# Second self attention of a perceiver block: exponentials and scores by halves of a group's four heads

## The reference

```python
q = split_heads(x @ Wq); k = split_heads(x @ Wk); v = split_heads(x @ Wv)   # b=2, h=16, s=256, d=16
qc = q - q.mean(axis=-1, keepdims=True)
kc = k - k.mean(axis=-1, keepdims=True)
cov = jnp.einsum('bhsd,bhtd->bhst', qc, kc) / D
var_comp = q_var[..., :, None] * k_var[..., None, :] / D
attn = jax.nn.softmax(cov + var_comp, axis=-1)
out = jnp.einsum('bhst,bhtd->bhsd', attn, v)
```

## Time and profile before

| what | value |
|---|---|
| median of three runs | 1666.3 us |
| the profiled execution's own time | 1669.16 us |
| its span in the profile | 1667.4 us |
| mean granted clock of TensorE | 0.961 |
| the eight steps of this self attention, first score to last division | 1561.30 to 1591.05 us |

### The profile page before, as it was taken

One profiled execution on the slowest core, in us unless ns is written; L12 is line 12 of the kernel. 1 busy time (PEld: TensorE's weight loads), 2 busy tenths in 40 slices (PEclk: granted clock), 3 DMA queues, 4 the chain that ended last, 5 costly groups with the idle time before them and its releaser, 6 DMA issues. The chain is left out here.

```text
span 1667.4 us, 42036 instructions
## 1 busy us (share of the span) xinstructions
PE 1547.2 (93%) x15983; PEld 874.4 (52%) x15983; DVE 1105.6 (66%) x1794; ACT 890.1 (53%) x1208; POOL 697.5 (42%) x543
## 2 busy tenths in 40 slices
PE   7999999999899999999878969999999999997783
PEld 3554545544333444433453426777777777774442
DVE  4656566566789999997337756666666666625446
ACT  5555555554378888888251015555555555552435
POOL 5431000000011111111153009999999999971710
PEclk9999999999799999999899969999999999998897
DMA  7988979886832222221400067555565565311000
GB/s 235 228 229 229 210 218 228 234 231 158 223 99 67 68 68 65 65 66 35 162 2 1 5 176 229 152 156 135 158 161 142 137 161 159 86 40 59 2 1 13
DMA packets 178503, 212.23 MB, mean 127 GB/s; under 512 B 57381, under 2 KB 151857, under 8 KB 173769
## 3 DMA queue, kind: packets, MB, share of 16 engines
q1 hardware_dynamic: 177800, 210.44, 46.3%
q10 hardware_dynamic: 576, 0.00, 0.0%
HBM read 122.78 MB, written 87.57 MB: 126 GB/s over the span
## 5 line engine op out<-in xcount | busy, mean ns | idle before, releaser
L1231 POOL TENSOR_TENSOR x_r<-x_p 128x1024 f16<-128x1024 f32 x256 | 478.9, 1895 | 6.3
L1246 DVE TENSOR_REDUCE x_mx<-a_all 128x2 f32<-128x1024 f32 x249 | 304.9, 1225 | 150.9 <-PE a_all L1129 150.9
L1206 ACT ACTIVATE x_p<-s_all 128x1024 f32<-128x1024 f32 x256 | 248.4, 1022 | 227.0 <-PE s_all L1112 227.0
L802 ACT ACTIVATE x_p<-s_all 128x1024 f32<-128x1024 f32 x256 | 261.6, 1025 | 60.8 <-PE s_all L709 55.4
L850 DVE TENSOR_REDUCE x_mx<-a_all 128x1 f32<-128x512 f32 x352 | 231.9, 682 | 15.2 <-PE a_all L718 8.3
L1112 PE MATMUL s_all<-x_q,x_k 64*128 64x256 f16 x3072 | 210.2, 269 | 0.0
L1147 PEld LDWEIGHTS o_all<-x_v,x_p 128*128 128x128 bf16 x2048 | 178.7, 97 | 40.1 <-issue 40.1
L1147 PE MATMUL o_all<-x_v,x_p 128*128 128x129 f16 x2048 | 197.3, 221 | 0.9 <-POOL x_r L1231 0.9
L1148 PE MATMUL o_all<-x_v,x_r 128*128 128x65 f16 x2048 | 192.5, 193 | 0.0
L1112 PEld LDWEIGHTS s_all<-x_q,x_k 64*128 64x128 f16 x3072 | 149.5, 94 | 62.2 <-issue 0.8
L1148 PEld LDWEIGHTS o_all<-x_v,x_r 128*128 128x128 f16 x2048 | 180.7, 98 | 0.0
(11 more groups left out here) (393 smaller groups left out, 2761.7 us busy)
## 6 DMA issues: line engine op xcount, KB each, us to landing
values<-vst SPq DMA_DIRECT2D x16, 2064.0 KB, 10.1
x_v<-values SPq DMA_DIRECT2D x32, 1032.0 KB, 5.3
keys<-kst SPq DMA_DIRECT2D x32, 1024.0 KB, 6.9
x_k<-keys SPq DMA_DIRECT2D x128, 256.0 KB, 5.2
wf<-keys SPq DMA_DIRECT2D x192, 64.0 KB, 2.1
values<-vst SPq DMA_DIRECT2D x16, 528.0 KB, 11.9
x_v<-values SPq DMA_DIRECT2D x32, 264.0 KB, 2.7
cf<-in_ctxT SPq DMA_DIRECT2D x16, 512.0 KB, 9.7
```

The costliest lines, as they stand in the source:

```text
L802: act.activation(prob[g % NP][:], chip.s_ps[g % 2][:].rearrange("p (c q) -> p c q", q=SQ), ACT.Exp, scale=hd ** -0.5).then_inc(p_ready, 1)
L1206: act.activation(prob[g % NP][:], chip.s_ps[g % 2][:].rearrange("p (c q) -> p c q", q=SQ), ACT.Exp, scale=hd ** -0.5).then_inc(p_ready, 1)
L1231: pool.tensor_tensor(rest[g % NP][:], prob[g % NP][:], hi, ALU.subtract).then_inc(rest_done, 1)
L1246: dve.tensor_reduce(mx[a[1] % 2][:, n // 4, 2 * (n % 4):2 * (n % 4) + 2], chunk_banks(u, g)[:, :].rearrange("p (h c) -> p h c", h=2), AX.X ...
```

## The change

With no mask, a step's four heads are worked as two halves, heads 0 and 1, then heads 2 and 3. `scores(i)` issues all 16 matmuls of the first half, announces them, then issues the 16 of the second half and announces those. The first half waits only for the exponential of the first half of step i-1. ScalarE does two exponentials over 1024 columns in place of one over 2048. `values(i)` waits for both. The masked self attention of the first layer keeps its instructions and their order.

```diff
-    EX = 2 if mask is not None else 1
+    EX = 2
+    halves = ((0, 1, 2, 3),) if mask is not None else ((0, 1), (2, 3))
...
-                    if i >= 1:
-                        pe.wait_ge(exp_done, EX * i)
-                    for kt in range(2):
...
-                        for part in range(4):
-                            for j in range(4):
...
-                    last.then_inc(s_ready, 1)
+                    for h, heads in enumerate(halves):
+                        if i >= 1:
+                            pe.wait_ge(exp_done, EX * i if mask is not None else EX * (i - 1) + h + 1)
+                        for kt in range(2):
...
+                            for part in range(4):
+                                for j in heads:
...
+                        last.then_inc(s_ready, 1)
...
-                        pe.wait_ge(exp_done, i + 1)
+                        pe.wait_ge(exp_done, EX * i + 2)
...
-                    act.wait_ge(s_ready, i + 1)
+                    if mask is not None:
+                        act.wait_ge(s_ready, i + 1)
                     if i >= 2:
                         act.wait_ge(pv_ready, i - 1)
                     if mask is None:
-                        act.activation(prob[i % 2][:], s_heads, ACT.Exp, scale=1 / 16).then_inc(exp_done, 1)
+                        for h in range(2):
+                            act.wait_ge(s_ready, 2 * i + h + 1)
+                            act.activation(prob[i % 2][:, 2 * h:2 * h + 2], s_heads[:, 2 * h:2 * h + 2], ACT.Exp, scale=1 / 16).then_inc(exp_done, 1)
```

More of the change, by code:

```diff
@@ L1770, in scores @@
                         pe.wait_ge(turn_copied, 1)
-                    if i >= 1:
-                        pe.wait_ge(exp_done, EX * i)
-                    for kt in range(2):
-                        q0 = first_query(kt)
-                        keys, queries = slice((2 * b + kt) * P, (2 * b + kt + 1) * P), slice(b * SQ + q0, (b + 1) * SQ)
-                        for part in range(4):
-                            for j in range(4):
[L1778 to L1785, removed]
@@ L1786, in scores @@
-                    last.then_inc(s_ready, 1)
+                    for h, heads in enumerate(halves):
+                        if i >= 1:
+                            pe.wait_ge(exp_done, EX * i if mask is not None else EX * (i - 1) + h + 1)
+                        for kt in range(2):
+                            q0 = first_query(kt)
+                            keys, queries = slice((2 * b + kt) * P, (2 * b + kt + 1) * P), slice(b * SQ + q0, (b + 1) * SQ)
+                            for part in range(4):
+                                for j in heads:
+                                    r, to = slice(32 * j, 32 * j + 32), s_heads[:, j, kt, q0:SQ]
+                                    if part == 0:
+                                        pe.matmul(to, ident[r, 32 * j + g:32 * j + g + 1].to_broadcast([32, P]), nmT[r, queries],
+                                                  start=(kt == 0), stop=False, skip_group_check=True)
+                                    else:
+                                        kp, qp = ((hi, hi), (hi, lo), (lo, hi))[part - 1]
+                                        last = pe.matmul(to, kp[1][r, g, keys], qp[0][r, g, queries],
+                                                         start=False, stop=(part == 3 and kt == 1), skip_group_check=True)
+                        last.then_inc(s_ready, 1)
```

## The result

The changed kernel takes 1668.43 us (median of 19 runs, 1666.82 to 1670.24), the kernel before 1665.74 us (19 runs). The ratio is 1.0015, 95% interval 1.0009 to 1.0021: 1.5 to 3.5 us slower, 2.5 us in the middle. Predicted were +1.8 us and 1668.1 us. The number came out nearly right. Its parts didn't, and the experiments are about these.

The account below looks back on a forecast made before the run. Bound: the loop scores, exponential, scores, with TensorE close behind. Scores(2) at 1568.3, five steps 17.45 and 4.19 us put values(7) at 1589.94 against 1588.19: +1.8 us, median 1668.1, range 1665.0 to 1671.5.

Parts of the forecast that it names:

- The bound: Attention steps: the loop scores, exponential, scores over one buffer sets 3.04 us; TensorE close behind, idle only 0.34 us.
- the very sum 0.98 + 1.00 + 0.64: TensorE's step: scores to values, values to turned output, turned output to next scores; 2.62 us if pairs cost half a four.
- The price of 0.109 us for a pair: Scores at full clock: two matmuls side by side take 0.109 us, from earlier pairs with 64 rows and 256 columns.
- The matmuls go as 16 pairs: Scores: 32 matmuls as 16 pairs, not 8 fours; 1.74 instead of 0.87 us, so steps of 3.49 us.
- The clock of the slow start: First attention steps: clock rises at 1566.4 us, following unbroken TensorE work from 1561.30; scores(2) start at 1568.3.
- my late end: Slow start, late case for the clock: scores(2) start at 1570.2 us, total +3.65 us.
- ScalarE: Attention steps: two exponentials take 1.94 us against 1.88, hidden; with the copy 2.3 us of work in 3.49.
- What follows is the same: Behind values(7): the attention's delay of +1.8 us goes through in full, with nothing else changed.
- Pairs by instructions: Scores: a pair costs half a four, TensorE's step is 2.62 us, total 1663.1 us; chance 0.06.
- Open weight loads: Scores: weight loads no longer hidden beside running matmuls, 0.16 us a pair, total 1675 us; chance 0.07.
- The change does nothing: Attention: extra time hidden by GpSimd's cover, or the whole drowned in later clock shifts and run spread; chance 0.06.
- The clock stays low: Attention: half-filled scores no longer raise the clock, a step takes about 6.8 us, total 1690 us; chance 0.03.

Follow-up runs that it names:

- The third buffer: Changed kernel, but scores by fours, exponentials still in halves, and three score buffers of two banks; ratio 0.9995 to the kernel before.
- exponentials in halves: Changed kernel with only the exponentials split; scores go by fours behind one wait as in the kernel before; ratio 1.0018 to the kernel before.
- the filled gap: Changed kernel plus five idle TensorE matmuls behind its last turned output, ahead of the projection; ratio 1.0015 to the kernel before.
- the mere delay: Kernel before plus one idle VectorE reduction (0.68 us) behind the attention's last division; ratio 1.0013 to the kernel before.

## Why the prediction came out as it did

*The bound (held).* TensorE was close behind the loop, the change removed its wait and filled the place with streaming. The third buffer shows it from the other side: the same split exponential with the streaming left whole and no buffer to wait for gives 2.62 us a step, the very sum 0.98 + 1.00 + 0.64. The price of 0.109 us for a pair was right too. Four matmuls in 0.11 us, where one takes 0.107 by its columns, is nearly four times the speed, and not just the 3.07 times with which the prediction had them agree.

*"The matmuls go as 16 pairs" (failed).* The number of slots was wrong: 12 in place of 16, as the second half starts before the first ends. That makes scores to values 1.44 and not 1.85 us, the step 3.08 and not 3.49, and the tail 3.78 and not 4.19. Five steps and the tail together were forecast 2.45 us too long. I had treated each half as a unit that ends before the next begins; with one head at a time, each head started when the one ahead had four matmuls left, and here the second half starts when the first has eight left, four in each of its two row groups.

*The clock of the slow start (failed).* I had it rise 5.1 us after the first score, as TensorE would work unbroken from there. It rose 9.2 us after it, where it rises in the kernel before (9.1). That is beyond my late end, and it is the prediction's own sign of being wrong, a rise after 1570 us, which is 8.7 us after the first score. Scores(2) started at 7.60 us, where I had 7.0; with 16 slots it would have been 8.9. Step 2 still ran mostly at the low clock and took 3.79 us, where I had 3.49. TensorE's work was unbroken but for one wait of 0.28 us (at 1560.36); why the rise didn't follow it is open.

*ScalarE (held).* Two exponentials took 1.94 us, hidden; the copy stayed off the path, and so did the division but for the tail. Its wait was not longer than before, though, as I had written, but the same.

*"What follows is the same" (failed).* The attention cost 0.6 us, not 1.8. The missing 1.4 us is in the down projection, one later rise of the clock, which comes with the delay. So two errors of opposite sign gave the right total, and that was luck. Four profiles with the first down matmul at 91.76 to 91.88 us (the changed kernel, exponentials in halves, the filled gap, the mere delay) take 16.3 us from there, with the rise 5.9 to 6.1 us after it; the kernel before has one profile without additions, with 14.9 us and the rise after 3.2 us. That the clock is the cause of the difference is shown by these profiles and, less sharply, by the times. Why the rise jumps by more than the delay is open.

*The rivals.* Pairs by instructions: excluded, a pair is 0.11 us. Open weight loads: excluded by the same rows. The change does nothing: excluded, the interval is clear of 1. The clock stays low: not in this kernel, but it is what happened with one head at a time. The prediction's reason against it was misread: the pairs of the earlier trace rows are of 64 rows each, in two different groups, so 128 rows were in use there and not the same 64.

## What to carry to other kernels

Matmuls with few rows run side by side when close neighbours in program order use different row groups; here TensorE reached past four waiting matmuls of a row group and no further. Cutting such a group in two to hand a half over sooner makes the half as slow as the whole. If the next engine waits for a first half, cut along what doesn't cost width, and look for a free buffer first. A change of half a microsecond can't be judged by its own stage: read the granted clock of every stage behind it, after TensorE's long idle times above all, and test with a pure delay. Idle matmuls that hold the clock up must end before the real operands come: here they gave back 0.3 to 1.3 us.

## What the runs showed of the hardware

- Matmuls of 32 rows start out of program order across row groups: with heads one after the other, each head starts when the one ahead has four matmuls left (0.83 us at 1.2 GHz, four slots of 0.21; 0.45 us at 2.4 GHz), and 32 matmuls take 20 slots. The page TensorE: Matmul & The Clock Gate of the Trainium skill (Part 3: Packing small matmuls) says that matmuls start in strict program order; here the trace disagrees.
- With one head at a time TensorE was busy 5.00 of 5.00 us in each stretch and was granted 1.2 GHz until 32.7 us after the first score, while its scores kept at most two of the four row groups at work; with pairs and a middle third of fours it was granted 2.4 GHz from 9.2 us. These are one profile each, and what made the difference was not tested.
- The clock's steps lay at the same place of the program in most profiles (first rise at 9.0 to 9.2 us from the first score in 9 of 13, the others at 8.2, 8.6, 12.0 and 32.7). Why so often the same stays open.
- The price of the low clock in the down projection: the part takes 13.3 us at 2.4 GHz, 14.9 us with the rise 3.2 us after its first matmul, and 16.3 us with the rise after 6.1 us.
